# Keeping each head of the second layer in the rows it was projected to, and laying out the beginning anew

## The reference

```python
x = x + A(layernorm(x));  x = x + F(layernorm(x))
# A: 16 heads; q = the normed x itself (8 columns a head), k = x@Wk+bk, v = x@Wv+bv (32 columns a head)
A(x) = x + gelu(softmax(q k^T + causal) v) @ Wf + bf
# F: 8 heads of 64 columns, 8 experts a head, one chosen by the largest gate
q, k = x@w_q, x@w_k;  gates = sigmoid(x@w_gate);  gm = one_hot(argmax(gates)) * gates
values = sum over e of gm[e] * (x @ value_experts[e])
out = softmax(causal(q*SCALE k^T)) values
F(x) = sum over heads and e of gm[e] * (out @ output_experts[e])
```

## Time and profile before

| | us |
|---|---|
| median of three runs | 1398.5 (1398.37 to 1403.59) |
| profiled execution: its own time | 1397.98 |
| profiled execution: span of the trace | 1395.9 |
| TensorE, VectorE, ScalarE, GpSimd busy in the span | 1165.2, 903.2, 894.2, 211.3 |
| mean granted TensorE clock | 0.960 of full |

### The profile page before, as it was taken

How to read it: one execution, slowest core, us unless ns; L and a number is a source line. 1 busy time by engine, 2 the same in 40 slices (tenths; PEclk the granted TensorE clock), 3 DMA queues, 4 the chain that set the end, 5 groups by cost and what they waited for, 6 DMA issues and landing times.

```text
span 1395.9 us, 19696 instructions
## 1 busy us (share of the span) xinstructions
PE 1165.2 (83%) x5720; PEld 644.5 (46%) x5720; DVE 903.2 (65%) x2786; ACT 894.2 (64%) x2551; POOL 211.3 (15%) x264
## 2 busy tenths in 40 slices
PE   2556988888988899888897898888898888978988
PEld 1114753356533564246642475335643356424753
DVE  5552857748575775747677585765858577674855
ACT  1694376935779266962769548793678827696370
POOL 3011011201112012020111102120111211111010
PEclk9987999999999999999999999999999999999999
DMA  2401733126421553206432073413642155320723
GB/s 78 132 2 63 179 93 91 37 68 149 113 56 34 123 130 99 60 6 153 118 82 62 25 177 89 95 32 82 148 105 52 34 140 128 84 62 11 175 67 71
DMA packets 64177, 122.32 MB, mean 88 GB/s; under 512 B 14099, under 2 KB 29843, under 8 KB 59683
## 3 DMA queue, kind: packets, MB, share of 16 engines
q1 hardware_dynamic: 58950, 87.50, 25.0%
q10 hardware_dynamic: 5120, 33.56, 10.8%
HBM read 61.11 MB, written 9.06 MB: 50 GB/s over the span
## 4 chain that ended last, share of the span: by engine, by line
PE 41%; DVE 20%; ACT 19%; issue 14%; POOL 3%; DMA 2%; SPq 1%; ACTq 0%; DVEq 0%; POOLq 0%
ACT masked L819 9%; ACT pt L877 8%; PE ps_m L605 7%; PE ps_o L596 7%; DVE masked L1103 6%; PE ps_m L431 3%; PE ps_exp L512 3%; PE ps_m L433 2%; PE ps_max L700 2%; PE ps_m L432 2%; PE ps_exp L513 2%; PE ps_exp L431 2%; POOL pt L999 2%; DVE val L1303 2%; DVE at L1153 2%
## 5 line engine op out<-in xcount | busy, mean ns | idle before, releaser
L1103 DVE CUSTOM_DVE_ANT_0 masked<-ps_max,mask 128x512 f32<-128x512 f32 (+3 forms) x768 | 353.1, 486 | 206.7 <-PE ps_max L511 92.1
L819 ACT ACTIVATE masked<-masked,low 128x512 f32<-128x512 f32 (+3 forms) x768 | 426.2, 558 | 72.2 <-DVE low L1103 68.1
L877 ACT ACTIVATE pt<-ps_exp 128x384 f32<-128x384 f32 (+1 forms) x480 | 248.0, 523 | 103.7 <-PE ps_exp L513 66.6
L999 POOL TENSOR_SCALAR_AFFINE_SELECT pt<-pt 128x512 f32<-128x512 f32 (+2 forms) x192 | 134.6, 701 | 709.2 <-ACT pt L877 709.2
L605 PE MATMUL ps_m<-at,oe_sb 128*128 128x512 f32 x416 | 219.9, 618 | 5.7 <-DVE at L1153 3.5
L596 PE MATMUL ps_o<-pt,val 128*32 128x128 f32 (+6 forms) x1536 | 185.5, 459 | 19.7 <-POOL pt L999 19.1
L511 PE MATMUL ps_exp<-s1q,s2k 96*128 96x384 bf16 (+3 forms) x384 | 103.6, 319 | 67.8 <-ACT pt L877 54.5
L511 PE MATMUL ps_max<-s2k,s1q 96*128 96x512 bf16 (+3 forms) x512 | 138.8, 320 | 21.0 <-DVE low L1103 11.9
L1153 DVE TENSOR_TENSOR at<-osb,hots 128x512 f32<-128x512 f32 x208 | 145.3, 704 | 15.7 <-PE ps_m L605 15.7
L819 ACT ACTIVATION_READ_ACCUMULATOR masked<-masked,low 128x1 f32 x768 | 149.4, 195 | 0.0
L511 PEld LDWEIGHTS ps_exp<-s1q,s2k 96*128 96x128 bf16 x384 | 32.6, 99 | 185.1 <-ACT pt L877 140.1
(11 more groups left out here) (159 smaller groups left out, 1837.9 us busy)
## 6 DMA issues: line engine op xcount, KB each, us to landing
hots<-hot_d ACTq DMA_DIRECT2D x64, 512.0 KB, 6.6
s1q<-pt SPq DMA_DIRECT2D x128, 128.0 KB, 2.3
s1k<-pt SPq DMA_DIRECT2D x128, 128.0 KB, 2.3
s1q<-parts_q SPq DMA_DIRECT2D x96, 96.0 KB
s2k<-parts_k SPq DMA_DIRECT2D x96, 96.0 KB
s2q<-pt SPq DMA_DIRECT2D x64, 128.0 KB, 2.3
s2k<-pt SPq DMA_DIRECT2D x64, 128.0 KB, 2.3
parts_q<-pt SPq DMA_DIRECT2D x24, 128.0 KB, 2.3
```

The costliest lines, as they stand in the source:

```text
L819: last = nc.scalar.activation(e, e, ACT.Exp, bias=low[:, g % 2, c:c + 1], scale=-1.0, accum_out=den[:, g % 2, c:c + 1])
L877: nc.scalar.activation(pt[:, (n % 2) * 4 + j, 0:c1 - c0], score_bank(k, u)[:, c0:c1], ACT.Exp).then_inc(exp_done[k].sem, 1)
L999: nc.gpsimd.affine_select(out=v, in_=v, compare_op=ALU.is_ge, fill=0.0, base=0, pattern=[[0, HG[k]], [0, m], [1, P]], channel_multiplier=- ...
L1103: last = v.tensor_tensor_reduce(out=masked[:, u % JUNK, c0:c0 + w], in0=src[:, c0:c0 + w], in1=mask[:, S - w:S], scale=-1.0, scalar=POS, o ...
```

## The change

The edits fall into four groups.

1. **Pairs of layer F.** A head keeps its rows. q high of head 2p+1 stays on rows 64 to 127 of `s1q` with its q low below it on rows 0 to 63, and so on. What stays in its rows is written there by an engine: GpSimd copies q high to `s1q` and k high to `s1k` (`copy_rows`, four copies a pair of 64x512), ACT copies q high to `s2q` (two copies a pair), VectorE writes k low straight into `s2k` in two instructions of 64 rows for one of 128. SP sends only what changes rows: q low and the second k high, four transfers a pair. TensorE waits for all of these (`stacks_made`). The rows of maxima and ones stand on rows 64, 65 for even heads and 0, 1 for odd ones, for which the final scores read all 128 rows, with rows 2 to 63 of `s2q` zero.
2. **Matmul rows.** Unshifted scores read 72 rows (A) or 64 (second product of F), the final ones 75 (A), 66 or 128 (F).
3. **Bytes and places of `hots`.** The choice is stored as bytes, in four buffers; ACT issues the reads at steps 2, 5, 8 and 11 of layer F, and none in layer A. The wait is on units of the batch before.
4. **The beginning.** The raw weights of layer F load right after those of layer A. Their split is done in the prologue. The three clearings of 128x4096 are gone; SP clears `s2q[0:64]` by a transfer of 1 MB from DRAM, issued after the constants have landed, and waits for it between the parts of q and those of k. The rows of ones of `ks` are sent with each group; the zero rows of `qs` no longer.

```diff
-SENDS = 12
+SENDS, COPIES = 4, 4
-HOTS_AT = {("F", 1): 0, ("F", 9): 1, ("A", 0): 2, ("A", 4): 3}
+HOTS_AT = {("F", 2): 0, ("F", 5): 1, ("F", 8): 2, ("F", 11): 3}
-        hots = sb("hots", [P, 2, E, S], BF16)
+        hots = sb("hots", [P, GROUPS, E, S], U8)
...
+            for dst, src in ((raw["wq"], wq), (raw["wkf"], wkf), (raw["wg"], wg),
+                             (ve_raw, ve.rearrange("p (e n) -> p e n", n=S))):
+                sp.dma_start(dst, src).then_inc(w_in[2].sem, 16)
             sp.dma_start(zeros_d, consts[5:9]).then_inc(cst.sem, 16)
...
-            sp.wait_ge(set_p.sem, set_p.count(0, 3))
...
+            sp.dma_start(s2q[0:64].bitcast(F32).rearrange("p h n -> p (h n)"), zeros_d[0].partition_broadcast(64)
+                         ).then_inc(zero_rows.sem, 16)
...
             def restack_f(f):
...
-                    sp.wait_ge(qk_lo.sem, qk_lo.count(f, 2 * p + 2))
-                    qh, ql, kh, kl = (pt[:, 4 * (p % 2) + n, :] for n in range(4))
-                    for ab in range(2):
-                        r, h = slice(64 * ab, 64 * ab + 64), 2 * p + ab
-                        for dst, src in ((s1q[0:64, h], qh), (s1q[64:128, h], ql), (s1k[0:64, h], kh),
-                                         (s1k[64:128, h], kh), (s2q[0:64, h], qh), (s2k[0:64, h], kl)):
-                            sp.dma_start(dst.bitcast(F32), src[r]).then_inc(pair_sent[p % 2].sem, 16)
+                    ql, kh = (pt[:, 4 * (p % 2) + n, :] for n in (1, 2))
+                    sp.wait_ge(qk_lo.sem, qk_lo.count(f, 2 * p + 1))
+                    for odd in range(2):
+                        sp.dma_start(s1q[ROWS[1 - odd], 2 * p + odd].bitcast(F32), ql[ROWS[odd]]
+                                     ).then_inc(pair_sent[p % 2].sem, 16)
+                    sp.wait_ge(qk_hi.sem, qk_hi.count(f, 2 * p + 2))
+                    for odd in range(2):
+                        sp.dma_start(s1k[ROWS[1 - odd], 2 * p + odd].bitcast(F32), kh[ROWS[odd]]
+                                     ).then_inc(pair_sent[p % 2].sem, 16)
...
             parts_to_dram(0, "q")
+            sp.wait_ge(zero_rows.sem, zero_rows.count(0, 16))
             parts_to_dram(0, "k")
...
+            def stacks_made(f, p):
+                pe.wait_ge(pair_sent[p % 2].sem, pair_sent[p % 2].count(f, 16 * SENDS * (p // 2 + 1)))
+                pe.wait_ge(rows_copied.sem, rows_copied.count(f, COPIES * (p + 1)))
+                pe.wait_ge(s2q_made.sem, s2q_made.count(f, 2 * (p + 1)))
+                pe.wait_ge(qk_lo.sem, qk_lo.count(f, 2 * p + 2))
...
-                if at_done.count(f, max(p - 1, 0) * E):
-                    act.wait_ge(at_done.sem, at_done.count(f, max(p - 1, 0) * E))
+                if f > 0:
+                    act.wait_ge(at_done.sem, at_done.count(f - 1, (p + 1) * E))
...
+                    if u % 2 == 1:
+                        p = u // 2
+                        qh = pt[:, 4 * (p % 2)].bitcast(F32R)
+                        act.wait_ge(qk_hi.sem, qk_hi.count(f, u))
+                        for odd in range(2):
+                            copy(s2q[ROWS[odd], 2 * p + odd], qh[ROWS[odd]]).then_inc(s2q_made.sem, 1)
...
+            def copy_rows(f, p):
+                qh, kh = (pt[:, 4 * (p % 2) + n].bitcast(F32R) for n in (0, 2))
+                pool.wait_ge(qk_hi.sem, qk_hi.count(f, 2 * p + 1))
+                for n, (dst, src) in enumerate(((s1q, qh), (s1k, kh))):
+                    if n == 1:
+                        pool.wait_ge(qk_hi.sem, qk_hi.count(f, 2 * p + 2))
+                    for odd in range(2):
+                        nc.gpsimd.tensor_copy(dst[ROWS[odd], 2 * p + odd], src[ROWS[odd]]).then_inc(rows_copied.sem, 1)
+                        pool.wait_ge(rows_copied.sem, rows_copied.count(f, COPIES * p + 2 * n + odd + 1))
...
-                    v.scalar_tensor_tensor(out=lo.bitcast(F32R), in0=ps_m[BANK[("F", "qk", u)]][:],
-                                           scalar=(SCALE, 1.0)[u % 2], in1=hi, op0=ALU.mult, op1=ALU.subtract
-                                           ).then_inc(qk_lo.sem, 1)
+                    src = ps_m[BANK[("F", "qk", u)]]
+                    if u % 2 == 0:
+                        v.scalar_tensor_tensor(out=lo.bitcast(F32R), in0=src[:], scalar=SCALE, in1=hi, op0=ALU.mult,
+                                               op1=ALU.subtract).then_inc(qk_lo.sem, 1)
+                    else:
+                        even, odd = ROWS
+                        v.tensor_tensor(s2k[even, u - 1], src[even], hi[even], ALU.subtract)
+                        v.tensor_tensor(s2k[odd, u], src[odd], hi[odd], ALU.subtract).then_inc(qk_lo.sem, 1)
...
-            v.memset(s1q[:].bitcast(F32), 0.0).then_inc(set_v.sem, 1)
```

More of the change, by code:

```diff
@@ L17 @@
 U32 = mybir.dt.uint32
+U8 = mybir.dt.uint8
 ALU = mybir.AluOpType
@@ L270, in build @@
         hot_out, at_done, at_used = sem("hot_out", 16), sem("at_done", T * E), sem("at_used", T * E)
-        hots_in = [sem(f"hots_in{n}", 2 * 2 * 16) for n in range(2)]
+        hots_in = [sem(f"hots_in{n}", 2 * 16) for n in range(GROUPS)]
         acc_copied, out_ready, y_done, y_out = (
@@ L352, in hots_to_dram @@
             def hots_to_dram(f):
                 sp.wait_ge(gmt_done.sem, gmt_done.count(f, 1))
-                if hots_in[1].count(f, 0):
-                    sp.wait_ge(hots_in[1].sem, hots_in[1].count(f, 0))
+                for arrived in hots_in:
+                    if arrived.count(f, 0):
+                        sp.wait_ge(arrived.sem, arrived.count(f, 0))
                 sp.dma_start(hot_d, gmt[:]).then_inc(hot_out.sem, 16)
@@ L505, in gates_transposed, with score @@
                 last.then_inc(gt_made.sem, 1)
-            def score(k, dst, h, rows, cols):
+            def score(k, dst, h, rows, cols, extra):
                 (l1, l2), (r1, r2) = rows, cols
                 if k == "A":
-                    return mm(dst, l1[0:KROWS, h, l2], r1[0:KROWS, h, r2], start=True, stop=True)
+                    n = STACK + PARTS if extra else STACK
+                    return mm(dst, l1[0:n, h, l2], r1[0:n, h, r2], start=True, stop=True)
+                n = (slice(0, 66), slice(0, P))[h % 2] if extra else ROWS[h % 2]
                 mm(dst, l1[0][:, h, l2], r1[0][:, h, r2], start=True, stop=False)
-                return mm(dst, l1[1][0:KROWS, h, l2], r1[1][0:KROWS, h, r2], start=False, stop=True)
+                return mm(dst, l1[1][n, h, l2], r1[1][n, h, r2], start=False, stop=True)
             Q = {"A": qs, "F": (s1q, s2q)}
@@ L727, in _ @@
             values_a(0)
-            pe.wait_ge(cst.sem, cst.count(0, 16 * 4))
-            pe.wait_ge(set_v.sem, set_v.count(0, 4))
-            pe.wait_ge(set_p.sem, set_p.count(0, 4))
+            pe.wait_ge(zero_rows.sem, zero_rows.count(0, 16))
+            pe.wait_ge(set_v.sem, set_v.count(0, 3))
+            pe.wait_ge(set_p.sem, set_p.count(0, 2))
             for b in range(B):
@@ L856, in attention @@
                         act.wait_ge(sent.sem, sent.count(b, 2 * 16 * SENDS))
+                    act.wait_ge(rows_copied.sem, rows_copied.count(b, 4 * COPIES))
                     if b + 1 < B:
@@ L1012, in _ @@
             inverse_deviation("A", 0)
-            nc.gpsimd.memset(s2q[:].bitcast(F32), 0.0).then_inc(set_p.sem, 1)
-            nc.gpsimd.memset(s2k[:].bitcast(F32), 0.0).then_inc(set_p.sem, 1)
             pool.wait_ge(set_v.sem, set_v.count(0, 2))
@@ L1022, in _ @@
                 inverse_deviation("F", b)
-                if b + 1 < B:
-                    inverse_deviation("A", b + 1)
+                for p in range(4):
+                    copy_rows(b, p)
+                    if p == 1 and b + 1 < B:
+                        inverse_deviation("A", b + 1)
                 gated_values(b)
@@ L1128, in negate @@
                 else:
-                    a = [nm_f[:, g % 2, 8 * n:8 * n + 8] for n in range(2)]
+                    a = [nm_f[:, g % 2].rearrange("p (j m t) -> p m j t", j=2, m=2)[:, n] for n in range(2)]
+                    r_jt = r.rearrange("p (j t) -> p j t", j=2)
                     dve.wait_ge(lng_made.sem, lng_made.count(b, 1))
@@ L1150, in choose @@
                     p = u // E
-                    dve.wait_ge(hots_in[p % 2].sem, hots_in[p % 2].count(f, 2 * 16 * (p // 2 + 1)))
+                    dve.wait_ge(hots_in[p].sem, hots_in[p].count(f, 2 * 16))
                     dve.wait_ge(sums_out["F"].sem, sums_out["F"].count(f, p + 1))
-                v.tensor_tensor(chosen_o(u), osb[:, u // E], hots[:, u // E % 2, u % E], ALU.mult
+                v.tensor_tensor(chosen_o(u), osb[:, u // E], hots[:, u // E, u % E], ALU.mult
                                 ).then_inc(at_done.sem, 1)
@@ L1179, in attention_a @@
                 for g in range(GROUPS):
-                    if g == SPLIT_AT and a == 0:
-                        expert_weights_low()
                     for s in range(STAGES):
@@ L1353, in _ @@
             values_a(0)
+            expert_weights_low()
```

76 lines of the change are left out of this document (36 added, 40 removed).

## The result

The changed kernel takes 1459.16 us (1455.89 to 1465.39, four runs) against 1398.43 (1395.87 to 1403.59, four runs) in the same comparison: ratio 1.0433, 95% interval 1.0398 to 1.0468. The prediction of 1390 and its range up to 1404 were wrong, with the wrong sign. The profiled execution after took 1458.64 us, its span is 1456.9.

What follows compares the result with a forecast made beforehand. It took TensorE and VectorE as nearly full in the later experts stage, TensorE as leading layer F and ACT layer A. From 1398, the beginning's -14 and eight batches' +6 gave 1390 us, range 1377 to 1404.

Steps and rivals of the forecast that it cites:

- The matmul rows change no column count: nothing either.: In the matmuls of layers A and F, reading other row counts was to cost nothing, as columns stay the same.
- ACT in pair 3: ACT's two copies a pair in the experts stage: taken as hidden, up to 1.2 us if cover in pair 3 is gone.
- k low in two instructions: VectorE in the experts stage: 0.6 us more a pair, 2.0 us a batch taken, ends 1.0 and 2.4.
- the rival in which the batches cost nothing: TensorE's existing waits absorb VectorE's extra and shrink by the clock: batch -1.5 to 0, 1384 in all; chance 0.28.
- Shared ports: GpSimd's copies block VectorE's gate chain through shared SBUF access: 0.4 us a batch, ends 0 and 1.5.
- the rival's point of decision of 1.8: Rival with port collisions at gate chain, normalisations and products: decides from 1.8 us a batch, 2.5 giving 1407; chance 0.15.
- The reads now come after those rows and are half the size: minus 1.2 a batch: In layer F, the `hots` reads were to follow group 1's rows of maxima, saving 1.2 us a batch, end 0.
- The minus 1.0 for the wait for `choose` in layer A: At layer A's step 0, ACT's 0.99 us hold was to go, saving 1.0 us for seven batches.
- the 32 transfers removed: SP's removed transfers, some 0.6 us each, were hidden before: nothing gained, up to 0.5 us a batch as a bound.
- The beginning: Before the batches: earlier rows of maxima -8, no weight split in layer A -7, +1: together -14 us, from -18 to -6.
- The bad end, constants at 24: At the start, slow loading puts constants at 24 us and zeros at 30, moving all by 8 us.
- The signs: Trace marks for right or wrong, such as first exponential near 56 and 0 to 2 us more between batches' residual additions.

Runs made afterwards that it cites:

- a_rows_full: The kernel after, with layer F's unshifted scores reading 66 or 128 rows instead of 64 and two more small clearing transfers a batch: 1445.02 us, ratio 1.0353.
- b_hots: The kernel before, with only the choice as bytes, four buffers and reads at steps 2, 5, 8 and 11 of layer F: 1414.55 us, ratio 1.0106.
- a_pool_klow: a_rows_full with k low in one instruction plus two transfers a pair, and GpSimd's 16 copies a batch as transfers again: 1403.08 us, one execution.

## Why the prediction was wrong, point by point

**The step that failed** is the sentence "The matmul rows change no column count: nothing either." Its price is 4.2 us a batch in the experts stage of after, and 52 us in all on the kernel before by itself. I had costed the matmuls by their columns alone, as if the overlap with their weight loads, which the 96-row products have, would stay. No rival had this mechanism, and no bad end covered it: all bad ends that I gave at once (k low 2.4, ports 1.5, ACT in pair 3 1.2, reads 0 and 1.5, layer A -1.0, beginning -6) make +5.6 a batch and 1437, under the 1459 measured. The +20 that the sum named as its upper end was narrower than its own terms.

**k low in two instructions**: "each pair adds 0.6, and a batch 2.4 ... I take 2.0". The mechanism and the place were right, the size was not: 4.5 to 4.8 a batch. The pair adds 0.8, since the 0.08 of overlap is left neither within it nor behind it. The larger part of the miss is the clock: longer waits account for 1.7 us a batch, close to the 2.0 taken, and the same matmuls at a lower clock for 2.9 to 3.1. I had counted the clock only as a gain (the rival in which the batches cost nothing).

**Shared ports**: 0.4 taken, ends 0 and 1.5; measured 1.2 to 1.8 (by one execution each), at the rival's point of decision of 1.8 but not over it. The copies take 0.64, as I took them, and each collision less than one copy.

**`hots`**: "The reads now come after those rows and are half the size: minus 1.2 a batch" was wrong in its first half. I read the order from the step numbers, not from the queues: ACT issues the reads at the head of the step in which it then copies `mt_f`. Alone this costs 4.6 us a batch between the third and fourth `mt_f`. In after it costs little (10.7 against 9.2): with the half-height products TensorE comes late enough to wait only 1.3 us there, at clock 1.00. Undo them, as a_rows_full does, and it comes out: 13.1, with 3.4 idle at clock 0.84 (read from the two traces, not from a run that changes `hots` alone). That is why mending the largest fault alone returned only 14 us; b_hots on the kernel before shows layer F longer by 4.2 from the places and bytes alone. What did come true is 0.7 us at the first group (11.5 to 10.8 between the first two `mt_f`). The minus 1.0 for the wait for `choose` in layer A came true in size (11.6 to 10.5) for another reason: it was the issue, not the wait. As predicted, the bytes didn't change `choose`, 0.68 us as before.

**Hidden as predicted**: the 32 transfers removed give nothing: a_pool_klow sends 24 more a batch than after, and its experts stage is within 0.3 us of that of before. ACT's copies cost 0.3 or nothing. No TensorE wait for a copy appears among the largest.

**The beginning**: -14 predicted, -17.5 measured, within its ends. The bad end, constants at 24, did not come.

**The signs**: the first exponential (54.28), the first maximum (34.98), the longer wait for low parts (2.4) and the gap of ACT came as written under "right"; the distance of the additions did not, 9.4 more instead of 0 to 2. Of the signs of being wrong, longer gate instructions appeared.

**The sum** over eight batches: experts stage 8 x 10.2 = 82, the rest of the batch 8 x (0.9 - 1.6) = -6, beginning -17.5, together +58; the spans differ by 61.

## What to carry to other kernels

Count a matmul's rows as a shape, not as a free size: look in the trace whether its weight load still runs ahead of it, and round 64 up to 65 or more where neighbours use the full array and the added rows can be zero on one side. Where an instruction is waited for by TensorE, price a longer wait for itself and for the clock behind it. And take the order of two transfers from the issue times in the timeline, of both queues, not from the steps at which the code names them.
